# Weight preparation of a self-attention stage: fourteen load buffers without a loop, the bias product between the transposes, the first layer norm beside them

## What is computed

```python
proj = layernorm(x) @ W_in.T + b_in        # W_in: 3072 x 512, q, k and v of 16 heads of 64
# rotary q and k, causal softmax(q k / 8) v  ->  y: 16 x 224 x 1024
x = x + y @ W_out.T + b_out                # W_out: 512 x 1024
```

## Time and profile before

| | us |
|---|---|
| median of 3 runs | 4072.93 |
| lowest, highest | 4070.74, 4074.32 |
| the profiled execution's own time | 4072.49 |
| its span in the profile | 4070.7 |

### The profile page before, as it was taken

How to read it: one execution, slowest core, us unless ns; L and a number is a source line. 1 busy time by engine, 2 the same in 40 slices (tenths; PEclk the granted TensorE clock), 3 DMA queues, 4 the chain that set the end, 5 groups by cost and what they waited for, 6 DMA issues and landing times. The chain is left out here.

```text
span 4070.7 us, 85297 instructions
## 1 busy us (share of the span) xinstructions
PE 3752.8 (92%) x28101; PEld 3217.9 (79%) x28101; DVE 2371.8 (58%) x5513; ACT 1741.6 (43%) x4280; POOL 1300.7 (32%) x1200
## 2 busy tenths in 40 slices
PE   6999999999679999999999998638999999999997
PEld 5888888888567887778877775637898898988986
DVE  4888888888546665666656664573434433334342
ACT  3545545555335555555555553103333333333332
POOL 1333333333225555555555554001102012022011
PEclk8999999999889999999999998558999999999998
DMA  3122222222233433334333431504333243233231
GB/s 110 50 61 60 56 56 65 52 61 52 91 97 99 108 101 95 103 103 107 101 96 102 103 90 49 148 6 112 94 98 111 76 117 111 80 109 111 85 99 53
DMA packets 319070, 354.23 MB, mean 87 GB/s; under 512 B 45135, under 2 KB 231991, under 8 KB 318996
## 3 DMA queue, kind: packets, MB, share of 16 engines
q1 hardware_dynamic: 309396, 325.67, 29.6%
q0 software_dynamic: 9600, 27.58, 2.4%
HBM read 189.05 MB, written 38.65 MB: 56 GB/s over the span
## 5 line engine op out<-in xcount | busy, mean ns | idle before, releaser
L1482 DVE TENSOR_REDUCE x_mx<-x_psS 112x1 f32<-112x752 f32 x512 | 481.4, 940 | 454.5 <-PE x_psS L1092 450.4
L2200 DVE TENSOR_TENSOR hid<-e_psU,act_g 128x280 f32<-128x280 f32 x256 | 115.1, 450 | 759.1 <-PE e_psU L34 759.1
L1330 ACT ACTIVATE x_pt<-x_psE 125x448 f32<-125x448 f32 x768 | 389.5, 542 | 324.5 <-PE x_psE L1104 318.7
L1004 POOL TENSOR_TENSOR part<-x_pt 125x448 f32<-125x448 f32 x256 | 292.5, 1142 | 608.7 <-ACT x_pt L1330 608.4
L2028 POOL TENSOR_TENSOR ex_y<-ex_y,ex_cur 112x2560 f32<-112x2560 f32 x8 | 45.5, 5691 | 1041.2 <-ACT ex_y L2176 1041.2
L562 POOL TENSOR_TENSOR qks<-qks,cos 128x448 f32<-128x448 f32 x128 | 147.8, 1154 | 699.1 <-DMA qks<-qk 699.1
L1092 PE MATMUL x_psS<-k_st,q_st 97*112 97x376 f32 x1024 | 284.7, 359 | 37.5 <-DVE x_mx L1482 22.9
L2133 ACT ACTIVATE act_g<-e_psG 128x280 f32<-128x280 f32 x256 | 103.6, 405 | 497.6 <-PE e_psG L34 497.5
L32 PE MATMUL e_psG<-ex_hi,g_hi 128*128 128x280 f32 x1024 | 299.6, 293 | 8.0 <-DVE g_lo L2194 6.7
L32 PE MATMUL pj<-xT_hi,win_hi 128*128 128x224 f32 x1024 | 303.1, 296 | 1.8 <-DVE xT_lo L634 1.7
L34 PE MATMUL e_psG<-ex_hi,g_lo 128*128 128x280 f32 x1024 | 298.9, 292 | 0.0
(11 more groups left out here) (280 smaller groups left out, 10847.8 us busy)
## 6 DMA issues: line engine op xcount, KB each, us to landing
k_st<-kT SPq DMA_DIRECT2D x768, 93.8 KB, 2.1
raw_g<-in_L_ffn_wg SPq DMA_DIRECT2D x128, 256.0 KB, 3.2
raw_u<-in_L_ffn_wu SPq DMA_DIRECT2D x128, 256.0 KB, 3.4
raw_d<-in_L_ffn_wd SPq DMA_DIRECT2D x128, 256.0 KB, 2.7
qks<-qk SPq DMA_DIRECT2D x512, 56.0 KB, 2.0
q_st<-qT SPq DMA_DIRECT2D x384, 56.0 KB, 2.0
ctxt<-in_ctx SPq DMA_DIRECT2D x16, 1125.0 KB
xt<-in_x SPq DMA_DIRECT2D x16, 448.0 KB, 3.6
```

The source lines that it names most:

```text
L1004: pool.tensor_tensor(part[:], pt[j][:, 0, :], pt[j][:, 1, :], ALU.add).then_inc(parted, 1)
L1330: act.activation(pt[j][:, i, :], psE[(j + i) % 2][0:KR, 0:2 * T], ACT.Exp, scale=XD ** -0.5).then_inc(exp_done, 1)
L1482: dve.tensor_reduce(mx[:, j, h:h + 1], psS[0:HT, :, 0:376], AX.XY, ALU.max).then_inc(s_taken, 1)
L2200: dve.tensor_tensor(h[i][:, halves[s]], psU[:, 0:CH], act_g[i][:, halves[s]], ALU.mult).then_inc(S["mul"], 1)
```

## The change

- The buffers `nat` grow from 4 to 14 and the PSUM banks of the turns from 4 to 6; two more banks, `psB` and `psO`, belong to the bias. All loops of the block are written out.
- The 8 tiles of W_out come first (u below 8), the 24 of W_in after them. SP issues the first eight tiles, then `xt`, then `bo`, then the other tiles; from tile 14 on it waits until tile u - 14 has been turned. The three tables follow after the last tile.
- b_in is turned before the first tile. The eight `mm3` of the bias product stand one each behind the turns 14 to 21, in a bank of their own. VectorE splits the spread bias between its fourth and fifth tile, and adds b_out after tile 28.
- VectorE does the four parts of the first layer norm after tiles 16, 18, 20 and 22. For this `xt`, `stats`, `mv`, `lnw`, `ssin`, `cos`, `mask`, four semaphores and the functions `at`, `norm_of` and `norm` move out of the second block.
- The second block's SP starts with `load_x(1)`, and VectorE's with `low_x` of the first batch.

What a tile's turn, copy and subtraction do, and all from the first projection on, is as it was. The diff, without the functions that only move:

```diff
-            nat = sb(c, "nat", [P, 4, D])
+            NATS, BANKS_W = 14, 6
+            nat = sb(c, "nat", [P, NATS, D])
-            ps = [c.enter_context(nc.psum_tensor(f"w_ps{i}", [P, 512], F32)) for i in range(4)]
-            nat_loaded = [sem(f"nat_loaded{i}") for i in range(4)]
+            ps = [c.enter_context(nc.psum_tensor(f"w_ps{i}", [P, 512], F32)) for i in range(BANKS_W)]
+            psB, psO = (c.enter_context(nc.psum_tensor(n, [P, 512], F32)) for n in ("w_psB", "w_psO"))
+            nat_loaded = [sem(f"nat_loaded{i}") for i in range(NATS)]
...
                 def _(sp):
                     sp.dma_start(ident[:], cst[:, 0:P]).then_inc(small_loaded, 16)
                     sp.dma_start(brow[:], b_in.rearrange("(c p) -> c p", p=P)).then_inc(small_loaded, 16)
+                    for u in range(8):
+                        sp.dma_start(nat[:, u, :], source(u)).then_inc(nat_loaded[u], 16)
+                    sp.dma_start(xt[:], at(xv, 0)).then_inc(x_loaded, 16)
                     sp.dma_start(bo[:], b_out.rearrange("(o n) -> o n", o=1).to_broadcast((HT, D))).then_inc(small_loaded, 16)
...
+                    for u in range(8, 32):
+                        if u >= NATS:
+
+                            sp.wait_ge(w_turned, u - NATS + 1)
+                        sp.dma_start(nat[:, u % NATS, :], source(u)).then_inc(nat_loaded[u % NATS], 16)
+                    sp.dma_start(ssin[:], cst[:, 128:352]).then_inc(const_loaded, 16)
+                    sp.dma_start(cos[:], cst[:, 352:576]).then_inc(const_loaded, 16)
+                    sp.dma_start(mask[:].rearrange("p a t -> p (a t)"), cst[0:HT, 576:1024]).then_inc(const_loaded, 16)
 
                 @block.tensor
                 def _(pe):
                     pe.wait_ge(small_loaded, 48)
...
+                    pe.transpose(psB[:, 0:24], brow[:], ident[0:24, 0:24]).then_inc(b_turned, 1)
+                    for u in range(32):
+                        pe.wait_ge(nat_loaded[u % NATS], 16 * (u // NATS) + 16)
+                        if u >= BANKS_W:
+                            pe.wait_ge(w_low, u - BANKS_W + 1)
                         for k in range(KD):
-                            m = pe.transpose(ps[s][:, k * P:(k + 1) * P], nat[:, s, k * P:(k + 1) * P], ident[:])
+                            m = pe.transpose(ps[u % BANKS_W][:, k * P:(k + 1) * P], nat[:, u % NATS, k * P:(k + 1) * P], ident[:])
                         m.then_inc(w_turned, 1)
...
+                        if u in range(14, 22):
+                            k = u - 14
+                            if k == 0:
+                                pe.wait_ge(b_spread, 4)
+                            m = mm3(pe, psO[0:HT, :], (bvb_hi[:, k, :], bvb_lo[:, k, :]), (wout_hi[:, k, :], wout_lo[:, k, :]),
+                                    k == 0, k == 7)
+                            if k == 7:
+                                m.then_inc(ob_done, 1)
...
                 @block.scalar
                 def _(act):
+                    for u in range(32):
+                        act.wait_ge(w_turned, u + 1)
+                        act.activation(split_to(u)[0], ps[u % BANKS_W][:].rearrange("p (k c) -> p k c", k=KD), ACT.Copy).then_inc(w_high, 1)
...
                 @block.vector
                 def _(dve):
+                    def low(u):
+                        hi, lo = split_to(u)
+                        dve.wait_ge(w_high, u + 1)
+                        dve.tensor_tensor(lo, ps[u % BANKS_W][:].rearrange("p (k c) -> p k c", k=KD), hi.bitcast(F32),
+                                          ALU.subtract).then_inc(w_low, 1)
+
                     dve.wait_ge(b_turned, 1)
...
+                    for u in range(4):
+                        low(u)
                     dve.wait_ge(b_spread, 2)
                     dve.tensor_copy(bvb_hi[:], bvb[:]).then_inc(b_spread, 1)
                     dve.wait_ge(b_spread, 3)
                     dve.tensor_tensor(bvb_lo[:], bvb[:], bvb_hi[:].bitcast(F32), ALU.subtract).then_inc(b_spread, 1)
-                    dve.wait_ge(ob_done, 1)
-                    dve.tensor_tensor(obias[:], ps[1][0:HT, :], bo[:], ALU.add).then_inc(b_spread, 1)
+                    for u in range(4, 32):
+                        low(u)
+                        if u in (16, 18, 20, 22):
+                            norm(dve, 0, (u - 16) // 2)
+                        elif u == 28:
+                            dve.wait_ge(ob_done, 1)
+                            dve.tensor_tensor(obias[:], psO[0:HT, :], bo[:], ALU.add).then_inc(b_spread, 1)
...
-                    sp.dma_start(xt[:], at(xv, 0)).then_inc(x_loaded, 16)
-                    sp.dma_start(ssin[:], cst[:, 128:352]).then_inc(const_loaded, 16)
-                    sp.dma_start(cos[:], cst[:, 352:576]).then_inc(const_loaded, 16)
-                    sp.dma_start(mask[:].rearrange("p a t -> p (a t)"), cst[0:HT, 576:1024]).then_inc(const_loaded, 16)
                     load_x(1)
...
-                    for part in range(4):
-                        norm(0, part)
                     for h in range(2):
                         low_x(0, h, pv[h])
```

More of the change, by code:

```diff
@@ L107, in self_attention, with at @@
         obias = sb(outer, "obias", [HT, D])
+        xt = sb(outer, "xt", [HT, 2, D])
+        stats, mv, lnw = sb(outer, "stats", [HT, 2, 6]), sb(outer, "mv", [HT, 2, 2]), sb(outer, "lnw", [HT, 8])
+        ssin, cos = sb(outer, "ssin", [P, T]), sb(outer, "cos", [P, T])
+        mask = sb(outer, "mask", [HT, 2, T])
+        gate, const_loaded, x_loaded, ln = (sem(n) for n in ("gate", "const_loaded", "x_loaded", "ln"))
+        xv = x.rearrange("b (h p) d -> b p h d", p=HT)
+        def at(view, b):
+            return view[b] if isinstance(b, int) else view[bass.ds(b, 1)].rearrange("o p h d -> (o p) h d")
@@ new lines, in norm_of @@
+        def norm_of(dve, src, dst, st, m_v, wk, done, n, part):
+            a, y, w = wk[:, 0:2], wk[:, 2:4], wk[:, 4:6]
+            if part == 0:
+                for h in range(2):
+                    dve.bn_stats(st[:, h, :], src[:, h, :]).then_inc(done, 1)
+            elif part == 1:
+                hold(dve, gate, done, n + 2)
+                for h in range(2):
+                    dve.bn_aggr(m_v[:, h, :], st[:, h:h + 1, :]).then_inc(done, 1)
+                dve.wait_ge(done, n + 4)
+                dve.tensor_scalar(w, m_v[:, :, 1], EPS, None, ALU.add).then_inc(done, 1)
+                dve.wait_ge(done, n + 5)
+                dve.tensor_scalar(y.bitcast(I32), w.bitcast(I32), 1, None, ALU.arith_shift_right).then_inc(done, 1)
+                dve.wait_ge(done, n + 6)
+                dve.tensor_scalar(y.bitcast(I32), y.bitcast(I32), -1.0, float(0x5F3759DF), ALU.mult, ALU.add).then_inc(done, 1)
+            elif part == 2:
+                for i in range(3):
+                    dve.wait_ge(done, n + 7 + 3 * i)
+                    dve.tensor_tensor(a, y, y, ALU.mult).then_inc(done, 1)
+                    dve.wait_ge(done, n + 8 + 3 * i)
+                    dve.scalar_tensor_tensor(a, a, -0.5, w, ALU.mult, ALU.mult).then_inc(done, 1)
+                    dve.wait_ge(done, n + 9 + 3 * i)
+                    dve.scalar_tensor_tensor(y, a, 1.5, y, ALU.add, ALU.mult).then_inc(done, 1)
+            else:
+                dve.wait_ge(done, n + 16)
+                for h in range(2):
+                    dve.tensor_scalar(dst[:, h, :], src[:, h, :], m_v[:, h, 0:1], y[:, h:h + 1], ALU.subtract,
+                                      ALU.mult).then_inc(done, 1)
@@ L110, in self_attention, with norm @@
+        def norm(dve, b, part):
+            if part == 0:
+                dve.wait_ge(x_loaded, 16 * b + 16)
+            norm_of(dve, xt, xt, stats, mv, lnw, ln, SLN_STEPS * b, part)
         with ExitStack() as c:
-            nat = sb(c, "nat", [P, 4, D])
+            NATS, BANKS_W = 14, 6
+            nat = sb(c, "nat", [P, NATS, D])
             brow = sb(c, "brow", [24, P])
@@ L120, in self_attention, with source, split_to @@
             wo_v = w_out.rearrange("(r p) (h k) -> r h p k", p=P, h=2)
-            def out_cols(u):
-                return slice(4 * (u % 2), 4 * (u % 2) + 4), slice((u // 2) * P, (u // 2 + 1) * P)
+            def source(u):
+                return wo_v[u // 2, u % 2, :, :] if u < 8 else w_in[(u - 8) * P:(u - 7) * P, :]
+            def split_to(u):
+                if u < 8:
+                    ks, cols = slice(4 * (u % 2), 4 * (u % 2) + 4), slice((u // 2) * P, (u // 2 + 1) * P)
+                    return wout_hi[:, ks, cols], wout_lo[:, ks, cols]
+                cols = slice((u - 8) * P, (u - 7) * P)
+                return win_hi[:, :, cols], win_lo[:, :, cols]
             with nc.Block() as block:
@@ L151, in turn @@
                         m.then_inc(w_turned, 1)
[L153 to L163, removed]
@@ L184, in _ @@
                 @block.vector
                 def _(dve):
[L186 to L192, removed]
@@ L584, in _ @@
```

(18 more changed lines are left out.)

50 lines of the change are left out of this document (5 added, 45 removed).

## The result

The changed kernel took 4050.24 us, median of five runs (4048.1 to 4056.7), beside 4072.43 us for the kernel before (4070.5 to 4074.3): ratio 0.995, 95% interval 0.9935 to 0.9964. That is 22.2 us less, where 20.6 were forecast, and 4050.2 lies inside the range. The five runs lie up to 8.6 us apart, so the two numbers agree more closely than the total can tell. The profiled execution, 4050.24 us, is the median one.

The account below looks back on a forecast made before the run. The unhidden head before the first projection was the bound: VectorE's end 43.0 + 0.3 + 3.2 = 46.5 us instead of 67.1, 20.6 us less, so 4052.3 us. Its own range was 4049 to 4056, the range given 4048.5 to 4059.

Parts of the forecast that it names:

- What bounds: the head, one to one: Before the first projection at 67.09 us: nothing hides the head, so moving that start moves the kernel's end as much.
- Start of TensorE: First block: TensorE's first wait includes bo, so it starts at 12.2 us, bounds 11.5 to 15.7, against 6.43 before.
- the part that loses: Load queue: bo behind eight tiles and xt makes TensorE's first wait cost 5.8 us against the start before.
- First low part: First block, VectorE: 3.3 us after TensorE's start plus 0.24 us for turning b_in, so at 15.7 us.
- VectorE's sum: First block: tiles, bias split, layer norm and last addition take VectorE 27.3 us, ending at 43.0 us without waits.
- TensorE close behind: First block: TensorE has 28.2 us of work, ends at 40.4 us at the earliest; VectorE is last.
- The ring of four as the pace of the kernel before: Weights before the change: four load buffers in 4.0 to 4.2 us set 1.0 to 1.05 us a tile.
- After the block: Crossing to the second block: barrier 0.28 us and 3.17 us from layer norm to first projection both remain.
- The rule against it: Turns in the first block: by the skill, transposes don't engage the full clock, so they would run low throughout.
- the first rival: First block: TensorE at 1.2 GHz becomes the bound; 4061.0 us in full, 4056 in part; chance 0.14.
- Rival 2: Loads: the DMA gets no faster, bo lands at 15.7 us at 250 GB/s, total 4055.8 us; chance 0.09 alone.
- rival 3: First block: written-out code arrives late, up to 5.8 us a stall; slower, say 4082 us; chance 0.04.

Follow-up runs that it names:

- e8: Changed kernel with b_out's one-row load replaced by 112 different rows of constants: first projection at 46.12 us against 46.24.
- e1: Changed kernel with the load of b_out issued ahead of the tiles: 4042.29 us, ratio 0.9929 to the kernel before; first projection at 39.51 us.
- e3: Changed kernel with the bias product in one piece behind all turns, b_out added at the end: first projection at 49.00 us against 46.24.
- e4: Changed kernel with the first layer norm and the loads of x and tables back in the second block: first projection at 52.47 us against 46.24.
- e6: Changed kernel with every mm3 of the bias product done twice, the second read by nobody: first projection at 52.22 us against 46.24.
- e7: Kernel before with its loops over the tiles written out and nothing else: first projection at 67.05 us against 67.09.
- e2: Changed kernel with 4 load buffers instead of 14, x and b_out behind the first four tiles: first projection at 48.54 us against 46.24.
- e10: e1 with 4 load buffers instead of 14: first projection at 47.99 us against 39.51.
- e11: Changed kernel with b_out loaded first, GpSimd spreading and splitting the bias and adding b_out, product between turns 10 to 17: 4045.50 us, ratio 0.9937.

## Why the prediction was right

By its steps:

- **What bounds: the head, one to one.** Right: 20.85 us of head, 22.3 of span, the difference within the scatter of the rest.
- **Start of TensorE** 12.2, measured 13.90. Wrong by 1.7 us, inside its bounds of 11.5 to 15.7. The step that failed is "the remaining 1.67 MB take 4.2 us at 400 GB/s", with a landing 1 us later. (By 7.0 us the slices of the earlier trace rows sum to 1.23 MB and not to 1.19; that is 0.1 us.) In the DMA view under e8 the 2.86 MB had been moved by 12.1 us instead of 11.2, with the stretch near 250 GB/s from 9.75 us on, and `bo` was seen 1.8 us after that instead of 1. Tiles issued behind it were moving by then; how much of the 1.8 us they took is not shown. I named the order as the part that loses; e1 shows what it lost, 6.7 us of head.
- **First low part** 15.7, measured 15.91, by luck: two errors cancel. The unrolled ScalarE loads its table at 0.76 us, not behind the first turn, so the 3.3 us from start to low part, and 0.24 for b_in, were 2.0 in all. Without this the forecast of the first projection, 46.5 against 46.24, would not have come out so close.
- **VectorE's sum** 27.3 us, measured 42.66 - 15.91 = 26.8, its waits included. Right, and e3, where the last low part comes no earlier without the product, agrees that VectorE set the pace. By little: with 5.0 us less for VectorE the block got only 1.6 us shorter (e4), so TensorE was the next bound just behind it.
- **TensorE close behind.** Right in kind, wrong in size: a free turn takes 3.48 / 7 = 0.50 us, not the 0.68 of a row with gaps of 0.2 to 0.3 us between the tiles' weight loads, so TensorE had more room over the whole block; and beside the product it had nearly none (e6).
- **The ring of four as the pace of the kernel before.** Borne out: e7 took away the loops without effect, and with the ring of four put back e2 and e10 had 1.06 and 1.15 us a tile. The kernel before was not run with a deeper ring alone.
- **After the block** 0.3 + 3.2 us, measured 46.24 - 42.66 = 3.6. Nothing was paid for the crossing.
- **The rule against it.** The Trainium skill, "TensorE: Matmul & The Clock Gate", section "Part 4: PE-mode transpose", has transposes not engage the full clock. From 14.13 to 24.3 us TensorE's only work was turns. The first four took 0.86 us each, as at 1.2 GHz in the earlier trace rows, which is seen from ScalarE waiting for each of them; of the 6.46 us of the first ten they leave 3.0 us to the other six, 0.51 us each:

```profile
16.13 0.60 ACT L224 ACTIVATE wout_hi<-w_ps 128x512 fp32r<-128x512 f32 x1 [0.26 <-PE w_ps L209]
...
16.99 0.60 ACT L224 ACTIVATE wout_hi<-w_ps 128x512 fp32r<-128x512 f32 x1 [0.26 <-PE w_ps L209]
...
17.84 2.67 ACT L224 ACTIVATE wout_hi<-w_ps 128x512 fp32r<-128x512 f32 x5 [0.26 <-PE w_ps L209]
```

From 33 to 36 us, again turns alone, it was 0.50 us a tile at a granted clock of 1.00. (The record says 1.00 for the first four turns too, which their pace contradicts.) The trace disagrees with the rule here, and so the first rival fell. Rival 2 happened in part, in the stretch in which x and `bo` were loaded; no stall of rival 3 is to be seen.

Split over the parts, each undone alone: norm and x 6.2 us, product between the turns 2.8 (1.6 at the first psY), ring 2.3 (with the earlier start that four buffers bring), banks 0.3, loops 0 (undone in the kernel before). The sum is 11.6 of 20.9. The rest shows in no single undoing. I put it down to W_out first with the bias split early, which e3 leaves in place, and to parts that cover for each other, as the square of ring and start shows; it was not isolated further.

## What to carry to other kernels

A wait on several loads is as late as the last of them: an engine's first wait should name only what it needs, and its loads should stand first in the queue (6.7 us here for moving one line). Undoing one part of a change measures it beside the others; a deep ring that brought 2.3 us where it also made the start later brought 8.5 once the start was early in either case. And room on an engine must be counted in the stretch where the work is put, not over the whole block.

## What the runs showed beside this

- A load of x (112 partitions, 0.459 MB) ahead of `bo` cost 1.91 us, 240 GB/s, between tiles of 128 partitions that moved at 366 to 404. `bo` covers 112 partitions too, and where it stood without x (e4) the rate still fell, to between 164 and 273 GB/s from 9.4 to 10.9 us. Why is open; another shape of these loads was not tried.
- GpSimd normalised x (two instructions with a scalar for each partition, 112x512) in 4.14 us where VectorE took 1.00; it subtracted 128x896 in 2.10 us against 1.09 and copied it in 0.93 against 0.63.
- The clock at the start of the batches is worth about a microsecond, by what TensorE did before: from first projection to first psY passed 24.8 us in e3, where the product had just run, and 26.0 in the changed kernel. In e11 it was 28.2, but the clock does not explain that: it was granted at 0.54 from 44 to 48 us and 1.00 after, so it rose some 6 us after the first projection, as in the changed kernel. TensorE waited 2.4 us for ScalarE's `pt` ahead of the first psY there, and 1.1 in the changed kernel; the rest is open.
- The part of the kernel that no version touches took 3997.9 to 4003.9 us, and five runs of one kernel lay up to 8.6 us apart, so one run of a version tells little below that by its total. Its timeline tells more, but a load's landing could lie 1.3 us off (e6).
